# Preparing all weights inside the first sequence's attention instead of ahead of it

## What is computed

```python
x = x + _L0_attn_ref(_layernorm(x), Wq, Wk, Wv, Wo)      # 16 heads, squared scores, causal
x = x + _L0_ffn_ref(_layernorm(x), w_gate, w_up, w_down)  # int8 weights, 768 hidden
x = x + _L1_attn_ref(_layernorm(x), norm_g, norm_b, ...)  # two Mamba scans, forward and backward
x = x + _L1_ffn_ref(_layernorm(x), w_gate, w_up, w_down)  # FP4 of weights and inputs, 704 hidden
```

## Time and profile before

| | us |
|---|---|
| median of 3 runs | 6630.95 (6627.23 to 6632.68) |
| the profiled execution, whole | 6625.01 |
| its span, first to last instruction | 6623.3 |
| first scan of sequence 0 (DVE L1267) | 281.10 |

### The profile page before, as it was taken

The page is one execution under the profiler, slowest core; times in us unless marked ns, Lnnn a source line. Parts: engine busy times, 40 slices in busy tenths (PEclk is TensorE's granted clock), DMA queues, the critical chain, the costliest instruction groups (busy, mean ns, idle before and its releaser), DMA issues. The chain is left out here.

```text
span 6623.3 us, 79907 instructions
## 1 busy us (share of the span) xinstructions
PE 4595.8 (69%) x21853; PEld 2953.3 (45%) x21900; DVE 4712.6 (71%) x6052; ACT 4210.5 (64%) x7080; POOL 4672.7 (71%) x2442
## 2 busy tenths in 40 slices
PE   5666677676777777676776777777677776767565
PEld 3344354443544444354443544444354444544443
DVE  4467686777768677686777768677686777768774
ACT  3476666667666666666667666666666667666562
POOL 0377767777777777767777876777777777776784
PEclk7787888888888888898888888888898888888777
DMA  3111111111111111111111111111111111111110
GB/s 114 37 36 47 42 52 41 52 46 34 58 40 47 43 54 50 39 50 42 51 46 34 60 38 47 46 50 51 39 50 43 52 44 40 54 39 42 43 44 27
DMA packets 152786, 308.71 MB, mean 47 GB/s; under 512 B 20870, under 2 KB 58310, under 8 KB 149926
## 3 DMA queue, kind: packets, MB, share of 16 engines
q1 hardware_dynamic: 152278, 302.80, 14.4%
HBM read 285.90 MB, written 16.84 MB: 46 GB/s over the span
## 5 line engine op out<-in xcount | busy, mean ns | idle before, releaser
L762 POOL TENSOR_TENSOR arena_m<-bS,arena_m 128x1024 f32<-128x1024 f32 x1024 | 2413.3, 2367 | 454.5 <-DMA bS<-brow 248.1
L1267 DVE TENSOR_TENSOR_SCAN arena_m<-psum,arena_m 128x512 f32<-128x512 f32 x2048 | 2437.4, 1209 | 161.1 <-ACT psum L990 125.3
L1564 PE MATMUL psum<-ident,arena_m 128*128 128x128 f32 x8192 | 1466.2, 316 | 1177.2 <-ACT hc L998 965.0
L1564 PEld LDWEIGHTS psum<-ident,arena_m 128*128 128x128 f32 x8192 | 1096.9, 162 | 1820.6 <-issue 1020.9
L990 ACT ACTIVATE psum<-arena_m,Aneg 128x512 f32<-128x512 f32 x2048 | 1414.6, 697 | 718.2 <-DVE arena_m L1267 695.3
L773 POOL TENSOR_TENSOR arena_m<-arena_m,hc 128x1024 f32<-128x1024 f32 x512 | 1212.8, 2369 | 460.2 <-ACT hc L998 354.7
L1278 DVE SCALAR_TENSOR_TENSOR arena_m<-psum,Ct,arena_m 128x512 f32<-128x512 f32 x1024 | 754.0, 737 | 681.3 <-PE psum L1564 679.0
L998 ACT ACTIVATE hc<-psum,Ct 128x512 f32<-128x512 f32 x1024 | 696.4, 680 | 38.9 <-PE psum L1564 38.6
L859 ACT ACTIVATE arena_a<-psum 128x512 f32<-128x512 f32 (+3 forms) x1024 | 380.3, 441 | 465.3 <-PE psum L1377 303.9
L1377 PE MATMUL psum<-arena_a 64*128 64x512 f32 (+3 forms) x2048 | 467.2, 562 | 160.0 <-ACT arena_a L859 56.4
L708 POOL TENSOR_SCALAR_AFFINE_SELECT arena_a<-arena_a 128x512 f32<-128x512 f32 x256 | 159.2, 637 | 540.5 <-ACT arena_a L859 540.5
(11 more groups left out here) (140 smaller groups left out, 7113.6 us busy)
## 6 DMA issues: line engine op xcount, KB each, us to landing
bS<-brow SPq DMA_DIRECT2D x512, 256.0 KB, 3.3
wB<-kept_B SPq DMA_DIRECT2D x16, 1408.0 KB, 6.2
wU<-kept_U SPq DMA_DIRECT2D x32, 512.0 KB, 5.6
wO<-kept_O SPq DMA_DIRECT2D x32, 512.0 KB, 5.7
wU<-kept_Z SPq DMA_DIRECT2D x32, 512.0 KB, 5.4
wA<-kept_A SPq DMA_DIRECT2D x16, 768.0 KB, 5.7
wB<-kept_B SPq DMA_DIRECT2D x16, 768.0 KB, 5.8
wA<-kept_A SPq DMA_DIRECT2D x16, 640.0 KB, 3.9
```

Source lines behind the costliest of these rows:

```text
L762: pool.tensor_tensor(hb[s % HBS][:, two, :], bS[:, s % 2, :].unsqueeze(1).to_broadcast([P, 2, T]), du[r][:, two, :], ALU.mult).then_inc(m_ ...
L1267: dve.tensor_tensor_scan(v, EB[j % EBS], v, 0.0, ALU.mult, ALU.add).then_inc(m_scan.sem, 1)
L1564: ins = pe.transpose(HT[i % 2][:, m * P:(m + 1) * P], hb[s % HBS][:, m, i * P:(i + 1) * P], ident[:, :])
```

## The change

All 40 jobs now lie in slots of b = -1. SP issues only the two norm vectors, then x and the four attention weights; all other loads stand behind them, at the last slot of b = -2. The order of jobs is turned round: int8 first (0 to 10, three casts in DVE's slots 4, 5, 6, jobs in slots 6 to 16), then Mamba (11 to 25, slots 28 to 42), then FP4 (26 to 39, slots 44 to 51 and two each in 57, 58, 59). The 54 operations of the quantiser are spread one by one over slots 10 to 52 instead of standing in six slots. The jobs use five banks in turn, those of the scan (`EB`, `HT`), which has not begun. Every job kind waits for its own load only. The store of the weights is split: int8 in slot 0 with a wait until it has landed, Mamba in slot 40, FP4 in slot 66; a wait for the Mamba stores stands in slot 77. Some buffers lie elsewhere (`s_fp4[0]` in `hc`, the third int8 array in `wA`, scales of the quantiser in `bS`). `Aneg` is computed in ACT's slot 45.

```diff
+        def second(b):
+            return isinstance(b, int) and b == -2
...
-        FRONT, FP4_IN, FP4_DVE, FP4_PE, FP4_OUT, FREE = 0, 2, 12, 36, 56, 92
+        INT8_OUT, MAMBA_OUT, FP4_OUT, KEPT, FREE = 0, 40, 66, 77, 92
+        CASTS = (4, 5, 6)
+        JOB_SLOT = list(range(6, 6 + NJ8)) + list(range(28, 28 + NJ - NJ8)) + [44, 45, 46, 47, 48, 49, 50, 51] + [57, 57, 58, 58, 59, 59]
+        FP4_SLOT = [10 + q * 43 // (6 * QOPS) for q in range(6 * QOPS)]
+        DECAYS = 45
...
+        def turned_in(b, j):
+            return [n for n in range(NJ4) if first(b) and JOB_SLOT[n] == j]
         def setup_bank(n):
-            return n % 8 if n < NJ else n % 3
+            return n % (EBS + 2)
...
+            def store_int8():
+                sp.wait_ge(setup_act.sem, NJ8 // 2)
+                sp.wait_ge(setup_dve.sem, (NJ8 + 1) // 2)
+                sp.dma_start(kept["A0"], d_gu0_flat).then_inc(stored8.sem, 16)
+                sp.dma_start(kept["B0"].rearrange("p (k n) -> p k n", k=NF), d_dn0).then_inc(stored8.sem, 16)
+                sp.wait_ge(stored8.sem, 16 * STORES8)
...
             def one(b):
                 for j in range(SLOTS):
-                    if first(b) and j == FRONT:
-                        store_weights()
-                        load_fp4()
+                    if first(b) and j == INT8_OUT:
+                        store_int8()
+                    if first(b) and j == MAMBA_OUT:
+                        store_mamba()
                     if first(b) and j == FP4_OUT:
                         store_fp4()
+                    if first(b) and j == KEPT:
+                        sp.wait_ge(stored.sem, 16 * STORES)
...
                     side("SP", work, b, j)
+                    if second(b) and j == SLOTS - 1:
+                        load_weights()
...
-            act.wait_ge(loaded["small"].sem, 16 * small_loads)
+            act.wait_ge(loaded["small"].sem, 16 * 2)
...
-            dve.wait_ge(loaded["ffn"].sem, 16 * 3)
-            for s in range(3):
+            def cast(s):
+                dve.wait_ge(loaded[f"cast{s}"].sem, 16)
                 dve.tensor_copy(s_flt[s], s_flt[s].bitcast(I32)).then_inc(cast_done.sem, 1)
-            for n in range(0, NJ, 2):
-                evict(n)
...
             def one(b):
                 for j in range(SLOTS):
-                    if first(b) and FP4_DVE <= j < FP4_DVE + 6:
-                        fp4_weights(j - FP4_DVE)
...
+                    if first(b) and j in CASTS:
+                        cast(CASTS.index(j))
+                    for n in turned_in(b, j - 1):
+                        if n % 2 == 0:
+                            evict(n)
+                    for q in range(6 * QOPS):
+                        if first(b) and FP4_SLOT[q] == j:
+                            fp4_weights(q)
...
-                old = n - (8 if n < NJ else 3)
+                old = n - (EBS + 2)
                 if old >= 0:
                     pe.wait_ge((setup_act if old % 2 else setup_dve).sem, old // 2 + 1)
...
-            for n in range(NJ):
-                turn_weights(n)
             pe.wait_ge(const_set.sem, 5 + G)
-            pe.wait_ge(setup_act.sem, NJ // 2)
-            pe.wait_ge(setup_dve.sem, (NJ + 1) // 2)
```

More of the change, by code:

```diff
@@ L205, in block_kernel @@
         SB = [psum[:, EBS + 2 + i, :] for i in range(3)]
-        loaded = {k: signal(f"loaded_{k}") for k in ("ffn", "mamba", "small", "fp4")}
+        loaded = {k: signal(f"loaded_{k}") for k in ("small", "vectors", "cast0", "cast1", "cast2", "mamba0", "mamba1", "fp40", "fp41", "fp42")}
         ones_set = signal("ones_set")
@@ L466, in block_kernel @@
         s_wout = [carve(arena_m, KD * DI, view="p (j k) -> p j k", j=KD) for _ in range(2)]
-        s_flt = [carve(arena_m, NF * D) for _ in range(3)]
         s_alog = carve(arena_m, 2 * NM * NS, view="p (r m n) -> p r m n", r=2, m=NM)
@@ L500, in block_kernel @@
                 for j0 in range(0, NF, 3):
-                    jobs.append(("cast", [(P, v[:, j, k * P:(k + 1) * P]) for j in range(j0, j0 + 3)],
+                    jobs.append((f"cast{s}", [(P, v[:, j, k * P:(k + 1) * P]) for j in range(j0, j0 + 3)],
                                  dst[:, k, j0 * P:(j0 + 3) * P], P))
@@ L504, in block_kernel @@
         for k0 in range(0, NF, 2):
[L505 removed]
+            jobs.append(("cast2", [(P, v[:, j, k * P:(k + 1) * P]) for k in (k0, k0 + 1) for j in range(KD)],
                          d_dn0[:, k0:k0 + 2, :].rearrange("p k c -> p (k c)"), P))
+        NJ8 = len(jobs)
+        for r in range(2):
+            for k in range(KD):
+                for j0 in range(0, 8, 4):
+                    jobs.append((f"mamba{r}", [(P, s_win[r][:, j, k * P:(k + 1) * P]) for j in range(j0, j0 + 4)],
+                                 d_win[r][:, k, j0 * P:(j0 + 4) * P], P))
+            jobs.append((f"mamba{r}", [(P, s_wx[r][:, m * P:(m + 1) * P]) for m in range(NM)],
+                         d_wx[r].rearrange("p m c -> p (m c)"), P))
+            for k0 in range(0, NM, 2):
+                jobs.append((f"mamba{r}", [(P, s_wout[r][:, j, k * P:(k + 1) * P]) for k in (k0, k0 + 1) for j in range(KD)],
+                             d_wout[r][:, k0:k0 + 2, :].rearrange("p k c -> p (k c)"), P))
+        jobs.append(("mamba1", [(P, s_wdt[:, m, :]) for m in range(NM)], wdtT[:, :], P))
         NJ = len(jobs)
@@ new lines, in load_weights @@
+                    sp.dma_start(s_wout[r], w["Wout"].rearrange("(j p) k -> p j k", p=P)).then_inc(loaded[f"mamba{r}"].sem, 16)
+                with nc.allow_non_contiguous_dma(reason="a few kilobytes of vectors"):
+                    for r in range(2):
+                        w = mamba[r]
+                        sp.dma_start(s_alog[:, r, :, :], w["Alog"].rearrange("(m p) n -> p m n", p=P)).then_inc(loaded["vectors"].sem, 16)
+                        sp.dma_start(convw[:, r, :, :], w["convw"].rearrange("(m p) o k -> p m (o k)", p=P)).then_inc(loaded["vectors"].sem, 16)
+                        for dst, n in ((convb, "convb"), (bdt, "bdt"), (Dp, "D")):
+                            sp.dma_start(dst[:, r, :], w[n].rearrange("(m p) -> p m", p=P)).then_inc(loaded["vectors"].sem, 16)
@@ L803, in evict @@
                 act.copy(dst, src).then_inc(setup_act.sem, 1)
-            for n in range(1, NJ, 2):
-                evict(n)
             def exponentials():
@@ L1082, in fp4_weights @@
                 half = cols // 2
-                dve.wait_ge(loaded["fp4"].sem, 16 * 3)
-                if part:
-                    dve.wait_ge(wquant.sem, QOPS * part)
-                for k in range(QOPS):
-                    quantise(s_fp4[s][0:rows, c * half:(c + 1) * half], wtmp[0:rows, 0:half], w_am, w_sc, w_inv, 0, wquant,
-                             QOPS * part, k)
+                if k == 0:
+                    dve.wait_ge(loaded[f"fp4{s}"].sem, 16)
+                    if part:
+                        dve.wait_ge(wquant.sem, QOPS * part)
+                quantise(s_fp4[s][0:rows, c * half:(c + 1) * half], wtmp[0:rows, 0:half], w_am, w_sc, w_inv, 0, wquant,
+                         QOPS * part, k)
             def norm_stat(n, b, src, k):
@@ L1568, in one @@
                 for j in range(SLOTS):
-                    if first(b) and 0 <= j - FP4_PE < NJ4 - NJ:
-                        turn_weights(NJ + j - FP4_PE)
+                    for n in turned_in(b, j):
+                        turn_weights(n)
                     tb, jt = spot(b, j - TURN)
```

97 lines of the change are left out of this document (40 added, 57 removed).

## The result

| | before | changed |
|---|---|---|
| median, us | 6631.30 (6627.23 to 6632.68, 4 runs) | 6577.93 (6576.31 to 6580.01, 4 runs) |
| profiled execution, us | 6625.01 | 6576.31 |
| its span, us | 6623.3 | 6574.6 |
| first scores of sequence 0 | 56.94 | 30.22 |
| fourth division | 152.44 | 101.07 |

The ratio of the changed kernel to the kernel before is 0.9921, interval 0.9904 to 0.9938: 53.4 us faster by the medians, 48.7 us by the two profiled executions.

A forecast was written before the change was run, and what follows sets the result against it. POOL's and DVE's scan work bounds the untouched steady part; the gain is on the chain to the first residual. Fourth division 54.3 us earlier, less 1.2 us for evictions, gives -53.1 us from 6630.95: 6578 us, range 6570 to 6593 us.

The forecast's parts named there:

- both holes: Before the first residual: x issued only at 23.28 us, and PE standing still 27.79 us for a division behind the quantiser.
- The head: Start of kernel: x loaded early, layer norm 28.9 us earlier, first scores at 30.2 us; late vectors cost 0 to 3.4 us.
- Jobs between scores: First attention: one job hides between two pairs of scores, two do not quite; +1.3 us (0 to 4).
- The clock: PE in the first attention: busier, so fewer pairs of scores at the 1.2 GHz level; -2.0 us (-5 to 0).
- The coupling: First attention: DVE, PE and ACT wait for one another slot by slot; +0.9 us (0 to 8), fourth division at 98.1 us.
- The walk down DVE's list: DVE's casts, evictions, quantiser operations and divisions added in order, giving the four divisions at 52.7, 70, 83.4 and 98.1 us.
- After the fourth division: Fourth division to residual: division near 98 us, residual near 103 us; the earlier trace had 152.44 and 157.12 us.
- Evictions in the layer norm: Slots 57 to 59, last six jobs: evictions on DVE inside the layer norm and on ACT; +1.2 us (0.4 to 2.5).
- B: Rival: PE at 1.2 GHz through the first two groups, DVE and PE in lockstep; gain about 41 us, 6590 us; chance 0.23.
- C: Rival: the standstill moves with the quantiser, only the head is gained; 28 us, 6603 us; chance 0.08 together with E.
- D: Rival: slots 6 to 52, evictions, quantiser operations and scores stop overlapping; 27 us slower, 6658 us; chance 0.03.
- E: Rival: SP's first wait, ahead of x, holds x, so the head is not gained; 6607 us; chance 0.08 together with C.

The follow-up runs named there:

- e1: The changed kernel with the quantiser's operations back in six slots (12 to 17), nine in each; 6597.84 us, ratio 0.9951 to the kernel before.
- e2: The kernel before with only the quantiser spread, over slots 12 to 42 instead of 12 to 17; 6603.03 us, ratio 0.9969 to the kernel before.
- e7: The changed kernel without the 54 operations of the quantiser, the FP4 weights used as they come; 6570.44 us.
- e6: The changed kernel with unread identity transposes on PE in slots 19 to 27, 49, 52 and 53, and jobs in four banks instead of five; 6571.57 us.
- e5: The changed kernel with ACT making all evictions of jobs 11 to 33, eleven fewer on DVE, no dummy work; 6574.26 us.
- e9: e6 with ACT also taking all evictions of jobs 24 to 33, five fewer on DVE; 6567.30 us, ratio 0.9906 to the kernel before.
- e8: The changed kernel with e3's slots, e5's evictions on ACT and dummy transposes on PE in slots 33 to 43, 49, 52 and 53; 6569.13 us.
- e3: The changed kernel with the 15 Mamba jobs ten slots earlier, in slots 18 to 32 instead of 28 to 42; 6577.86 us.

## Why the prediction was right, and where it was off

The time was predicted at 6578 us and came at 6577.93 us. The mechanism is shown: both holes close, each by its own edit (e1, e2), and the gain is kept through all sequences. But that the figure agrees to a tenth of a microsecond is luck: against its own profiled execution the forecast was 53.1 us and 48.7 us came. The residual came at 108.35 us (near 103 said) and the first scan at 232.86 us (near 228 said). Of the 4.4 us between 53.1 and 48.7, 3.0 are missing in the attention and 2.6 in the step behind it; 1.2 come back, 0.7 between residual and first scan and 0.5 behind it. Medians of one kernel moved by up to 7.7 us (before) and 5.7 us (changed) between sets of runs, and this covered the 4.4 us.

- *The head.* Right. Layer norm 5.94 us (6.3 said), first scores 30.22 us (30.2 said). The two parts of it were each off by half a microsecond or less. The late vectors (up to 3.4 us) did not come: ACT's wait ended at 3.60 us.
- *Jobs between scores.* Said +1.3 us. Not separable from the clock in any run; 67.3 us in e7, with all jobs and one slow stretch, against 67.7 us for the attention of before without its standstill, bounds their cost, less what the clock gave back, near zero.
- *The clock.* Said -2.0 us (-5 to 0), with a granted clock near 1.00 from 30 to 100 us. The two levels came, the place did not: the first group came back to 1.00, the second fell to 0.52. The stage would have been 1.9 us shorter at 1.00 throughout (e6). The prediction also set down what follows from the Trainium skill, page "TensorE: Matmul & The Clock Gate", section "Part 1: The HAM clock gate (the "warmup" mystery)", alone: activity releases the throttle, so all 5 us would come back. In the change they did not; with more work for PE in e6 the clock held at 1.00 until behind the residual, which agrees.
- *The coupling.* Said +0.9 us (0 to 8), fourth division at 98.1 us; it came at 101.07 us. This is the term that failed in size. The walk down DVE's list gave divisions at 52.7, 70, 83.4 and 98.1 us; they came at 53.46, 71.99, 87.09 and 101.07 us. The list itself was right: DVE did not lack time (e5). What the walk left out is that an operation of DVE can stretch one of POOL's: the masks took 4.5 us more, of which PE waited for 1.5, and the last division started 1.4 us behind its data, where the walk had 0.9. e7 puts all of the quantiser at 3.6 us, e6 the slow clock at 1.9 us; how the missing 3.0 us divide between the two is not shown.
- *After the fourth division.* Taken from the earlier trace rows as 4.68 us, came as 7.28 us. The step that failed is that the duration of a row was moved without its clock: in before this stretch ran at 1.00, in the change at 0.50 from 101.7 us on (e6, e9: 4.67 and 4.68 us at 1.00 and 0.94). Both kernels have jobs on PE shortly ahead; what differs is the division behind DVE's late operations and PE's wait of 2.21 us in place of 0.87. So the late division may have its share here too.
- *Evictions in the layer norm.* Said +1.2 us. Gain at the residual 48.8 us, at the first scan 48.2 us: 0.5 us.
- *Rivals.* B's mechanism (slow clock, lockstep) came in one group of two and with the clock low for 14 us (50.5 to 64.1), in place of both groups. C is what e1 shows, 25.8 us for the head alone where 28 us were said. D and E did not come: PE's longest wait in the attention was 2.05 us and x was SP's third load.

Both medians of the change (6577.93 and 6572.24 us) lie between 6570 and 6593 us.

## What to carry to other kernels

Work that is off the chain in sum can still hold it in one place: spread it in pieces small enough that no operation others wait for stands behind more than one of them, and read the walk engine by engine, with the operations that stretch one another. A duration from a trace holds with its clock; before it is moved, look at how long PE will stand still ahead of the place it is moved to. Where PE has little to do on a chain that waits for it, cheap extra products can be worth more than they cost: 3.5 to 4.8 us here at the first scan (e6).

## What the runs showed of the hardware

- POOL's mask of 128x512 f32 takes 0.63 us alone and up to 1.6 us beside operations of the quantiser on DVE; with these left out all 16 took 634 to 637 ns. In the change all nine stretched masks ended 0.49 to 0.50 us behind the end of a DVE operation (TENSOR_TENSOR, TENSOR_SCALAR or SCALAR_TENSOR_TENSOR; the mask that began beside the reduction L1073 was not stretched). The DVE operation is stretched too where a mask was first, from 1.22 to 1.53 us.
- PE busy 5.98 of 10 us was followed by a granted clock of 0.52 (twice, in the change and its repetition: 5.51 of 10 us, then 0.50), while with 7.27 of 10 us (e6) it stayed at 1.00. e8 at 8.29 and e3 at 7.52 of 10 us still fell to 0.83 and 0.66 in the next stretch, so the share of busy time alone doesn't tell it.
- An issue of a DMA of 64 KB on SP took 11.37 us (11.4 to 11.8 us in the nine other runs with the order of the change) with some 7 MB issued ahead of it, where the issue of x takes 0.46 us. The cause is not shown: in the kernel before no issue of the first 30 us takes over 2.4 us.
